# A mixture-of-experts and attention kernel: sine and amplitude rows behind the logits, expert loads re-ordered around the first gather, tile rows turned ahead of the gate products, one hidden copy a step later

## The chip, the cores and the metric

The kernel runs on one core of a Trainium2 chip. The engines have names in the profile: PE is TensorE (matrix products; PEld are its weight loads), DVE is VectorE, ACT is ScalarE, POOL is GpSimd, SP is SyncE, which issues most transfers. The metric is device time in microseconds (us), the median of several runs.

## The reference, cut to what matters

```python
xn = layernorm(x)                                   # x: 8 batches x 512 rows x 256
# attention: q, k, v, o are low rank: (xn @ basis.T) @ (amp * cos(phase)).T, 32 harmonics, 16 heads
attn_out = holo(softmax(q @ k.T * scale) @ v, "o")
# experts: 8 experts, the best 2 for each row, hidden width 352
scores = softmax(xn @ gate_w.T);  top 2, normalised, times 2.5
expert = silu(x @ w_gate[e]) * (x @ w_up[e]) @ w_down[e]
# a shared expert of hidden width 704 for every row
shared = silu(xn @ sw_gate) * (xn @ sw_up) @ sw_down
out = x + attn_out + expert_sum + shared
```

## The kernel before, in words

Each engine has its own program, written out by hand. Semaphores tie them together: an engine runs its list in order, and a wait holds everything behind it. A float32 value is split into a high part (rounded to the format that TensorE multiplies) and a low part, and each product is made of three. So every weight needs a copy on ACT (the high part, `high_part(e)`) and a subtraction on DVE (the low part, `low_part(e)`).

The work goes through these stages.

1. **Rows and logits.** For each of 8 batches ACT normalises 4 tiles of 128 rows (`normal(b)`), PE turns them (`turn_rows`), ACT copies the high part of the turned columns (`columns_high`), DVE subtracts the low one (`columns_low`), PE makes the router's logits (`logits(b)`), ACT copies them (`keep_logits`), PE turns them back (`turn_logits`). On the side the cosines of the low-rank weights are made: `angles()` on DVE, a sine on ACT, `thrice()` on DVE (amplitude times sine, three copies), `turn_thrice()` on PE into PSUM banks, two copies `w_rows` on ACT and `small_rows()` on DVE.
2. **Routing.** DVE alone finds the two best experts of each row (to `hot_b`), PE counts them, DVE works out slots.
3. **Token list.** For each batch DVE writes two one-hot arrays (`one_hots`: `at_tile1`, `at_row`), ACT scales one by the token numbers (`token_ids(b)`), and PE sums 8 small products into one bank (`invert(b)`). The arrays have two buffers, so that batch b waits for batch b-2. Then DVE casts the bank to `token_of`, and `a_done` is raised. In the same stretch PE and ACT make the low-rank rows of the first attention batch (`project_first`, `rest_first` on PE, `project_high`, `project_low` on ACT).
4. **Expert tiles.** POOL gathers 128 rows for each of 71 tiles by `token_of`, four ahead. For tile s PE turns the rows (`turn_x`), ACT and DVE split them (`x_out`, `x_low`), PE makes gate and up products (`gate_up`, 12 products of 352 columns), ACT and DVE make the hidden values (`silu`, `hidden`), PE turns them (`turn_h`) and makes `down` (9 products of 256 columns). The order on PE is gate_up(s), turn_x(s+1), turn_h(s-1), down(s-2). The first 8 tiles wait for `lo_dve`, one expert for each. The rest run in a loop of 8 tiles.
5. **Attention and shared expert.** 8 batches x 4 groups x 8 steps. In a step ACT takes the exponent of 1024 scores (`exponent`, one PSUM pair `st_pair`, so that the next `score_T` on PE waits for it), DVE the maxima of the next group, and PE fills in products of the shared expert. The hidden rows of that expert come in blocks. Block 1 (`BOTH`, 64 rows) is gated in step 5 of group 1, and ACT copies its high part (`hidden_high`) one step later.

SP's list sets the order of the transfers. `KEPT` is 6: experts 0 to 5 are loaded in front of the `qk_rows` stores (the first attention batch), experts 6 and 7 once the first gather has landed (`c_x[0]`), into a buffer of their own.

## Time and profile before

| | us |
|---|---|
| median of 3 runs (lowest, highest) | 1013.65 (1013.43, 1014.67) |
| the profiled execution: time, span | 1018.13, 1016.3 |
| PE busy | 931.1 (92%) |
| DVE, ACT, POOL busy | 641.8, 570.7, 310.5 |
| mean granted TensorE clock | 0.95 of full |

The span runs from the first to the last instruction; the time is 1.83 us more. Rows of a timeline begin with the start and the duration, and a number in square brackets behind a row is how long the engine stood idle before it, and on what. The granted clock is a share of 2.4 GHz: 1.0 is that, 0.50 is 1.2 GHz.

### The profile page before, as it was taken

To read this page: it belongs to the slowest core of one execution; us is meant where nothing else is said; L and a number is where in the kernel's file an instruction comes from. 1 tells how busy PE (TensorE), PEld (TensorE's weight loads), DVE (VectorE), ACT (ScalarE), POOL (GpSimd) and SP (SyncE) were. 2 spreads that over 40 slices of the span, in tenths; PEclk is the share of its full clock that TensorE was granted. 3 is DMA by queue.
4 is the path that set the end of the run, shared out by engine and by line. 5 is a ranking of instruction groups with operands and counts; after the bars stand their busy time and mean duration, and the time that the engine had idled before them with its cause. 6 is when DMAs were issued, how large, how long until landed. Compare 5 with 4: busy or idle time off the path is not lost.

```text
span 1016.3 us, 17567 instructions
## 1 busy us (share of the span) xinstructions
PE 931.1 (92%) x5563; PEld 610.3 (60%) x5564; DVE 641.8 (63%) x978; ACT 570.7 (56%) x900; POOL 310.5 (31%) x297
## 2 busy tenths in 40 slices
PE   4755999999999968899999999999999999999998
PEld 2445999999999952345545545545545545545546
DVE  7777744334444446666776776676776776786753
ACT  5756544444444434556566566566566566665563
POOL 1003222222222106135235235135235235135232
PEclk9765999999999985799999999999999999999999
DMA  9977255222222235354565465565565565544220
GB/s 317 363 232 270 83 161 144 72 72 67 76 67 69 63 114 160 104 137 139 156 165 147 148 156 143 160 148 147 165 150 135 174 147 143 170 105 96 57 63 22
DMA packets 94079, 139.90 MB, mean 138 GB/s; under 512 B 18200, under 2 KB 51488, under 8 KB 92992
## 3 DMA queue, kind: packets, MB, share of 16 engines
q1 hardware_dynamic: 87328, 121.25, 41.6%
q0 software_dynamic: 6480, 17.70, 5.9%
q8 instruction: 36, 0.59, 0.2%
q14 instruction: 27, 0.22, 0.1%
q10 hardware_dynamic: 208, 0.14, 0.0%
HBM read 79.24 MB, written 54.71 MB: 132 GB/s over the span
## 4 chain that ended last, share of the span: by engine, by line
PE 66%; DVE 12%; issue 8%; ACT 8%; DMA 2%; POOL 2%; SPq 2%; ACTq 0%; POOLq 0%
PE bank L1335 9%; PE st_pair L1346 8%; PE bank L1241 8%; PE s_pair L1223 7%; PE bank L1401 7%; PE st_pair L1223 7%; PE bank L1358 6%; PE s_pair L1297 5%; ACT prob L1023 4%; DVE top L1727 4%; PE bank L1231 2%; DVE h_f L1751 2%; PE bank L1206 2%; ACT x_n L834 1%; PE bank L1368 1%
## 5 line engine op out<-in xcount | busy, mean ns | idle before, releaser
L1727 DVE TENSOR_REDUCE top<-s_pair 128x2 f32<-128x1024 f32 x252 | 308.6, 1225 | 149.7 <-PE s_pair L1297 148.5
L1023 ACT ACTIVATE prob<-st_pair 128x1024 f32<-128x1024 f32 x256 | 260.7, 1018 | 174.9 <-PE st_pair L1346 173.0
L758 POOL TENSOR_TENSOR h_T<-h_f,h_T 128x512 fp32r<-128x512 f32 x40 | 51.4, 1285 | 364.6 <-ACT h_T L1005 364.6
L736 POOL DMA_INDIRECT xg<-xn_rows,token_of x71 | 70.0, 986 | 269.8 <-PE bank L1206 187.5
L1346 PEld LDWEIGHTS st_pair<-q_rows,k_rows 50*128 50x128 f32 x512 | 49.1, 188 | 168.2 <-ACT prob L1023 122.4
L1346 PE MATMUL st_pair<-q_rows,k_rows 50*128 50x512 f32 x512 | 131.7, 510 | 15.9 <-ACT prob L1023 10.4
L1335 PE MATMUL bank<-xT_b,w_sh 128*128 128x512 f32 x528 | 145.7, 411 | 0.0
L1358 PE MATMUL bank<-prob,v_ones 128*32 128x512 f32 x1024 | 140.7, 622 | 0.0
L1297 PE MATMUL s_pair<-k_rows,q_rows 48*128 48x512 f32 x504 | 113.7, 443 | 6.3 <-DVE top L1727 5.7
L1335 PEld LDWEIGHTS bank<-xT_b,w_sh 128*128 128x128 f32 x528 | 94.1, 191 | 31.4 <-issue 12.0
L1241 PE MATMUL bank<-w_exp,c_hT 128*128 (+1 forms) x639 | 93.6, 291 | 1.0 <-ACT c_y L946 1.0
L1223 PE MATMUL s_pair<-w_exp,xg_T 128*128 x432 | 78.1, 331 | 11.1 <-issue 9.8
L1401 PE MATMUL bank<-w_sh,h_T 128*128 128x256 f32 (+1 forms) x544 | 84.4, 297 | 0.1
L1241 PEld LDWEIGHTS bank<-w_exp,c_hT 128*128 128x128 f32 (+1 forms) x639 | 80.6, 190 | 1.4 <-issue 1.4
L1401 PEld LDWEIGHTS bank<-w_sh,h_T 128*128 128x128 f32 (+1 forms) x544 | 71.5, 190 | 12.7 <-DVE h_f L1751 3.5
L1223 PEld LDWEIGHTS s_pair<-w_exp,xg_T 128*128 128x128 f32 x432 | 70.3, 192 | 13.5 <-issue 13.5
L1223 PE MATMUL st_pair<-w_exp,xg_T 128*128 x420 | 74.8, 328 | 1.2 <-DVE xg_T L1690 1.2
L1223 PEld LDWEIGHTS st_pair<-w_exp,xg_T 128*128 128x128 f32 x420 | 68.4, 192 | 1.6 <-issue 1.5
L1681 DVE TENSOR_TENSOR c_h<-c_sil,s_pair 128x352 f32<-128x352 f32 x36 | 18.8, 521 | 79.7 <-PE s_pair L1223 77.7
L1297 PEld LDWEIGHTS s_pair<-k_rows,q_rows 48*128 48x128 f32 x504 | 50.5, 193 | 27.4 <-DVE top L1727 16.4
L769 POOL DMA_INDIRECT y_b<-expert_rows,slot_of x64 | 61.1, 955 | 18.4 <-issue 17.7
L1681 DVE TENSOR_TENSOR c_h<-c_sil,st_pair 128x352 f32<-128x352 f32 x35 | 18.2, 521 | 64.0 <-PE st_pair L1223 63.8
(226 smaller groups left out, 1143.4 us busy)
## 6 DMA issues: line engine op xcount, KB each, us to landing
qk_rows<-qk_hi SPq DMA_DIRECT2D x56, 256.0 KB
q_rows<-qk_rows SPq DMA_DIRECT2D x64, 192.0 KB
k_rows<-qk_rows SPq DMA_DIRECT2D x56, 192.0 KB
expert_rows<-c_y SPq DMA_DIRECT2D x71, 128.0 KB, 1.7
xn_T_split<-x_T SPq DMA_DIRECT2D x8, 1024.0 KB, 5.6
xT_b<-xn_T_split SPq DMA_DIRECT2D x32, 256.0 KB, 4.7
qk_rows<-qk_lo SPq DMA_DIRECT2D x28, 256.0 KB
x_all<-in_L_attn_x_dram SPq DMA_DIRECT2D x8, 512.0 KB, 8.1
```

What stands on the lines that cost most here:

```text
L736: pool.indirect_dma_start(xg[s % 4][:, :], None, xn_dram, bass.IndirectOffsetOnAxis(token_of[:, s:s + 1], 0)).then_inc(c_x[s % 4], 16)
L758: pool.tensor_tensor(h_T[0:m, LO, f, :], h_f[q % 2][0:m, :], h_T[0:m, HI, f, :].bitcast(F32), ALU.subtract).then_inc(p_h, 1)
L769: pool.indirect_dma_start(y_b[:, t, k, :], None, y_dram, bass.IndirectOffsetOnAxis(slot_of[:, k, of(b) * TPB + t:of(b) * TPB + t + 1], 0)) ...
L1023: act.activation(prob[kt % 2][:, 2 * jp:2 * jp + 2, :].rearrange("p j l -> p (j l)"), st_pair[:, :], ACT.Exp, scale=HD ** -0.5).then_inc(a ...
L1223: ins = pe.matmul(gu_bank[i % 2][n][:, 0:F], xg_T[i % 2][:, a * KT + k, :], w, start=(m == 0 and k == 0), stop=(m == 2 and k == KT - 1))
L1241: ins = pe.matmul(y_bank[:, 0:D], c_hT[i % 2][0:n, a, k, :], w, start=(m == 0 and k == 0), stop=(m == 2 and k == FT - 1))
L1297: ins = pe.matmul(score_pair(b, g, v)[:, i * 512:(i + 1) * 512], q_rows[g][r:r + 48, jp, qt * P:(qt + 1) * P], k_rows[g][r:r + 48, jp, :], ...
L1335: ins = pe.matmul((g_bank, u_bank)[n][:, :], w_sh[:, a, o:o + P], xT_bs[b % 3][:, c, k, :], start=(i == 0), stop=(i == 5))
L1346: ins = pe.matmul(st_pair[:, i * 512:(i + 1) * 512], k_rows[g][r:r + QK_ROWS, jp, kt * P:(kt + 1) * P], q_rows[g][r:r + QK_ROWS, jp, :], s ...
L1358: ins = pe.matmul(ot_bank[32 * j:32 * j + 32, :], v_ones[:, kt, 4 * g + j, :], prob[kt % 2][:, j, :], start=(kt == 0), stop=(kt == TPB - 1))
L1401: ins = pe.matmul((g_bank, u_bank)[t % 2][:, 0:D], h_T[0:m, a, f, t * P:(t + 1) * P], w_sh[0:m, c, S_GU + f * D:S_GU + (f + 1) * D], start ...
L1727: dve.tensor_reduce(top[g % 2][:, :, jp, qt], score_pair(b, g, v)[:, :].rearrange("p (i k) -> p i k", i=2), AX_X, ALU.max).then_inc(d_max, 1)
```

## The change

Seven things are edited.

- The sine goes behind `keep_logits(6)`. `turn_thrice` goes behind the first low-rank products on PE, into banks 4 and 5, the `w_rows` copies behind `e_lo` on ACT, and `small_rows` behind `hot_b` on DVE.
- SP loads expert 0 ahead of the first low-rank rows, and `high_part(0)` comes before the first projections.
- `token_ids(0)`, `token_ids(1)` on ACT and `invert(0)`, `invert(1)` on PE go in between the last projections.
- `EARLY` is 4: experts 4 to 7, not 6 and 7, are loaded behind the first gather, and their high parts follow the first four tiles on ACT.
- PE turns tile s+1 ahead of gate_up(s), ACT and DVE split it ahead of silu(s) and hidden(s).
- `hidden_high(BOTH)` comes one step later in the attention.

```diff
+        EARLY = NE - 4
+        def unit_two(b, g, t):
+            return (b, g, t - 2) if t >= 2 else after(b, g, -1) + (STEPS - 2 + t,)
+        thrice_bank = [bank[4], bank[5]]
@@ SP
             sp.wait_ge(consts, 1)
+            load_expert(0)
...
-            for e in range(KEPT):
+            for e in range(1, EARLY):
                 load_expert(e)
...
             sp.wait_ge(c_x[0], 16)
-            for e in range(KEPT, NE):
+            for e in range(EARLY, NE):
                 load_expert(e)
@@ ACT
             normal(7)
-            act.wait_ge(angle_ok, 1)
-            act.activation(angle, angle, ACT.Sin).then_inc(sin_done, 1)
             columns_high(6)
...
             keep_logits(6)
-            act.wait_ge(pe_prep, 2)
-            for i in range(2):
-                ins = act.activation(w_rows[...], bank[i][0:96, :], ACT.Copy)
-            ins.then_inc(rows_hi, 1)
+            act.wait_ge(angle_ok, 1)
+            act.activation(angle, angle, ACT.Sin).then_inc(sin_done, 1)
             keep_logits(7)
...
             act.activation(e_lo[0][0:96, :], rest_bank[0:96, :], ACT.Copy).then_inc(d_r, 1)
+            (the w_rows copies, from thrice_bank)
+            high_part(0)
...
             project_low(2)
+            token_ids(0)
             project_high(3)
+            token_ids(1)
             project_low(3)
-            high_part(0)
-            for b in range(NB):
+            for b in range(2, NB):
                 token_ids(b)
...
             def step(s, i, first=False, last=False):
-                silu(s, i)
                 if not (last and i == END - 1):
                     x_out(s + 1, (i + 1) % 4)
+                silu(s, i)
...
-                    if what == "up" or what == "gate" and i == BOTH:
+                    what, c, i = unit(*unit_two(b, g, t)) if t else (None, None, None)
+                    if what == "gate" and i == BOTH:
+                        hidden_high(c, i)
+                    what, c, i = unit_before(b, g, t)
+                    if what == "up":
                         hidden_high(c, i)
@@ PE
             low_rank_first()
+            turn_thrice()
             pe.wait_ge(hot_ok, 1)
...
+            invert(0, 0, first=True)
             project_first(3)
+            invert(1, 1)
             rest_first(3)
...
+                    if not (last and i == run - 1):
+                        turn_x(s + i + 1, (i + 1) % 4)
                     gate_up(s + i, i, at[i + 2])
-                    if not (last and i == run - 1):
-                        turn_x(s + i + 1, (i + 1) % 4)
@@ DVE
             columns_low(7)
-            small_rows()
...
             dve.tensor_tensor(hot_b[:, :, :], ...).then_inc(hot_ok, 1)
+            small_rows()
             dve.wait_ge(count_ps, 1)
...
             def step(s, i, first=False, last=False):
-                hidden(s, i)
                 if not (last and i == END - 1):
                     x_low(s + 1, (i + 1) % 4)
+                hidden(s, i)
```

Three places of the order are shown, each as it stood and as it stands.

ACT at the end of the first stage, before: the lines are those of the kernel before; `raw_all` is the sine's operand, `lg_rows` are the copies of `keep_logits`, `x_T` the two copies of `columns_high`.

```order
L870 ACT_TABLE_LOAD
L870 ACTIVATE raw_all<-raw_all 128x256 [waits angle_ok]
L842 ACTIVATE x_T<-st_pair 128x512 [waits xT_stored2,lg_turned,xt_ps]
L842 ACTIVATE x_T<-st_pair 128x512
L873 ACTIVATE neg<-ident_f 128x128 [waits consts]
L848 ACTIVATE lg_rows<-bank 16x512 [waits lg_ps,lg_turned]
L842 ACTIVATE x_T<-bank 128x512 [waits xT_stored3,lg_turned,xt_ps]
L842 ACTIVATE x_T<-bank 128x512
L848 ACTIVATE lg_rows<-bank 16x512 [waits lg_ps,lg_turned]
L879 ACTIVATE w_rows<-s_pair 96x512 [waits pe_prep]
L879 ACTIVATE w_rows<-s_pair 96x512
L848 ACTIVATE lg_rows<-bank 16x512 [waits lg_ps,lg_turned]
```

The same place in the changed kernel:

```order
L848 ACTIVATE x_T<-st_pair 128x512 [waits xT_stored2,lg_turned,xt_ps]
L848 ACTIVATE x_T<-st_pair 128x512
L854 ACTIVATE lg_rows<-bank 16x512 [waits lg_ps,lg_turned]
L848 ACTIVATE x_T<-bank 128x512 [waits xT_stored3,lg_turned,xt_ps]
L848 ACTIVATE x_T<-bank 128x512
L879 ACTIVATE neg<-ident_f 128x128 [waits consts]
L854 ACTIVATE lg_rows<-bank 16x512 [waits lg_ps,lg_turned]
L882 ACT_TABLE_LOAD
L882 ACTIVATE raw_all<-raw_all 128x256 [waits angle_ok]
L854 ACTIVATE lg_rows<-bank 16x512 [waits lg_ps,lg_turned]
```

The table load and the sine have moved from ahead of the last columns to ahead of the last `lg_rows` copy, and the `w_rows` copies are gone from here.

PE around the last projections and the token list, before: `at_tile,at_row` are the products of `invert`, eight for a batch.

```order
L1172 MATMUL st_pair<-e_hi,neg 128x512 [waits a_qk] x2
L1172 MATMUL bank<-x_T,neg 128x512 [waits a_qk]
L1167 MATMUL bank<-e_qk,w_rows 128x512 [waits d_qk]
L1168 MATMUL st_pair<-e_qk,w_rows 128x512
L1172 MATMUL st_pair<-x_T,neg 128x512 [waits a_qk]
L1181 MATMUL st_pair<-at_tile,at_row 128x72 [waits d_qk,inv_ok,inv_row]
L1181 MATMUL st_pair<-at_tile,at_row 128x72 x7
```

The same place in the changed kernel:

```order
L1179 MATMUL st_pair<-e_hi,neg 128x512 [waits a_qk] x2
L1179 MATMUL bank<-x_T,neg 128x512 [waits a_qk]
L1188 MATMUL st_pair<-at_tile,at_row 128x72 [waits d_qk,inv_ok,inv_row]
L1188 MATMUL st_pair<-at_tile,at_row 128x72 x7
L1174 MATMUL bank<-e_qk,w_rows 128x512 [waits d_qk]
L1175 MATMUL st_pair<-e_qk,w_rows 128x512
L1188 MATMUL st_pair<-at_tile,at_row 128x72 [waits inv_ok,inv_row]
L1188 MATMUL st_pair<-at_tile,at_row 128x72 x7
L1179 MATMUL st_pair<-x_T,neg 128x512 [waits a_qk]
```

The fourth projection now stands behind the first batch's token products, and its rest behind the second's.

ACT in steps 4 to 7 of group 1 of an attention batch, before: `prob` are the exponents of steps 5, 6 and 7, `h_T<-h_f 64x512` is `hidden_high(BOTH)`.

```order
L1023 ACTIVATE prob<-st_pair 128x1024 [waits b_st]
L988 ACTIVATE top_T<-bank 8x512 [waits m_in0,b_mt]
L999 ACTIVATE h_f<-bank 64x512 [waits p_h,b_g]
L1023 ACTIVATE prob<-st_pair 128x1024 [waits b_st,b_pv]
L1005 ACTIVATE h_T<-h_f 64x512 [waits b_dn,d_hf]
L1023 ACTIVATE prob<-st_pair 128x1024 [waits b_st]
```

The same place in the changed kernel:

```order
L1028 ACTIVATE prob<-st_pair 128x1024 [waits b_st]
L993 ACTIVATE top_T<-bank 8x512 [waits m_in0,b_mt]
L1004 ACTIVATE h_f<-bank 64x512 [waits p_h,b_g]
L1028 ACTIVATE prob<-st_pair 128x1024 [waits b_st,b_pv]
L1028 ACTIVATE prob<-st_pair 128x1024 [waits b_st]
L1010 ACTIVATE h_T<-h_f 64x512 [waits b_dn,d_hf]
```

The exponent of step 7 and the copy have changed places.

## Rows read from the trace of the kernel before

**Rows 1.** Busy time in two stretches: engine busy and instructions, clock, DMA share.

```profile
200.00:300.00 100.00, 96.39 (x704) 95.24 (x703) 40.24 (x81) 45.37 (x108) 25.35 (x28) 1.00 0.22 71
...
657.92:734.35 76.43, 74.80 (x436) 38.91 (x434) 56.24 (x69) 47.53 (x63) 28.46 (x26) 1.00 0.58 157
```

**Rows 2.** Timeline of ACT at the end of the first stage.

```profile
40.58 1.28 ACT L870 ACT_TABLE_LOAD   x1
...
42.20 1.06 ACT L842 ACTIVATE x_T<-st_pair 128x512 fp32r<-128x512 f32 x2
```

**Rows 3.** Timeline of PE there: logits, turned logits, `turn_thrice` (L1102).

```profile
39.54 1.11 PE L1120 MATMUL bank<-x_T,gate_T 128*16 128x512 f32 x4
...
43.97 0.61 PE L1128 MATMUL bank<-ident_f,lg_rows 16*128 16x16 f32 x4 [2.26 <-ACT lg_rows L848]
44.64 1.89 PE L1120 MATMUL bank<-x_T,gate_T 128*16 128x512 f32 x4
46.33 1.91 PE L1102 MATMUL s_pair<-ident_f,raw_all 128*96 128x128 f32 x8
...
48.70 1.85 PE L1120 MATMUL bank<-x_T,gate_T 128*16 128x512 f32 x4
```

**Rows 4.** Busy time from 44 to 46 us, columns as above.

```profile
44.00:46.00 2.00, 1.94 (x8) 0.98 (x9) 2.00 (x4) 0.87 (x2) 0.00 (x0) 0.50 0.68 254
```

**Rows 5.** Timeline of DVE: `small_rows`, the first logits row, the counted totals.

```profile
49.38 1.28 DVE L1563 TENSOR_TENSOR w_rows<-s_pair,w_rows 32x512 fp32r<-32x512 f32 x2 [2.73 <-ACT w_rows L879]
51.68 0.69 DVE L1603 TENSOR_REDUCE lg<-bank 128x256 f32<-128x512 f32 x1 [1.02 <-PE bank L1128]
...
61.23 0.42 DVE L1620 COPY totals<-s_pair 128x256 f32<-128x256 f32 x1 [0.70 <-PE s_pair L1189]
```

**Rows 6.** Timelines of ACT, DVE and PE in the token list.

```profile
68.05 2.01 ACT L821 ACTIVATE w_exp<-w_exp 128x2176 fp32r<-128x2176 f32 x1
69.96 2.54 ACT L905 ACTIVATE at_tile<-at_tile,token_id 128x144 fp32r<-128x144 f32 x8
...
66.67 0.76 DVE L1654 TENSOR_TENSOR at_tile<-iota_s,slot_q 128x576 f32<-128x576 f32 x1
...
71.37 14.44 PE L1181 MATMUL st_pair<-at_tile,at_row 128*128 128x72 f32 x64 [3.85 <-DVE at_row L1656]
...
86.27 0.23 DVE L1671 CAST token_of<-st_pair 128x72 int32<-128x72 f32 x1
```

**Rows 7.** Timelines of POOL, DVE and PE at the first gather, and landing times of ten gathers.

```profile
86.79 3.29 POOL L736 DMA_INDIRECT xg<-xn_rows,token_of  x1 [81.34 <-DVE token_of L1671]
90.39 1.81 POOL L736 DMA_INDIRECT xg<-xn_rows,token_of  x1 [0.30 <-issue]
...
86.62 4.76 DVE L1575 TENSOR_TENSOR w_exp<-w_exp 128x2176 fp32r<-128x2176 f32 x2
...
94.37 0.66 PE L1206 MATMUL bank<-ident_f,xg 128*128 128x128 f32 x2 [8.55 <-DMA xg<-xn_rows,token_of]
...
DMA to landing us min/median/max: 2.6/5.2/7.4
```

**Rows 8.** Timeline of PE, gate products of tiles 0 to 2; landing of experts 6, 7.

```profile
96.21 3.88 PE L1223 MATMUL s_pair<-w_exp,xg_T 128*128 x12 [1.18 <-DVE xg_T L1690]
...
101.67 3.69 PE L1223 MATMUL st_pair<-w_exp,xg_T 128*128 x12 [1.15 <-DVE xg_T L1690]
...
106.65 2.20 PE L1223 MATMUL s_pair<-w_exp,xg_T 128*128 x12 [0.75 <-issue]
...
DMA to landing us min/median/max: 4.3/6.0/7.8
```

**Rows 9.** Timelines of ACT, DVE and PE at step 7 of group 1, fourth attention batch.

```profile
660.95 0.63 ACT L1005 ACTIVATE h_T<-h_f 64x512 fp32r<-64x512 f32 x1 [1.56 <-DVE h_f L1751]
...
660.94 1.23 DVE L1727 TENSOR_REDUCE top<-s_pair 128x2 f32<-128x1024 f32 x1
...
662.63 0.50 PE L1346 MATMUL st_pair<-q_rows,k_rows 50*128 50x512 f32 x2 [0.90 <-ACT prob L1023]
```

More of the change, by code:

```diff
@@ L868, in _ @@
             normal(7)
+            columns_high(6)
+            keep_logits(5)
+            columns_high(7)
+            act.wait_ge(consts, 2)
+            act.activation(neg[:, :], ident_f[:, :], ACT.Copy, scale=-1.0)
+            keep_logits(6)
             act.wait_ge(angle_ok, 1)
             act.activation(angle, angle, ACT.Sin).then_inc(sin_done, 1)
-            columns_high(6)
-            act.wait_ge(consts, 2)
-            act.activation(neg[:, :], ident_f[:, :], ACT.Copy, scale=-1.0)
-            keep_logits(5)
-            columns_high(7)
-            keep_logits(6)
-            act.wait_ge(pe_prep, 2)
-            for i in range(2):
-                ins = act.activation(w_rows[:, 2 * i:2 * i + 2, :].rearrange("p n d -> p (n d)"), bank[i][0:96, :], ACT.Copy)
-            ins.then_inc(rows_hi, 1)
             keep_logits(7)
@@ L888, in _ @@
             act.activation(e_lo[0][0:96, :], rest_bank[0:96, :], ACT.Copy).then_inc(d_r, 1)
+            act.wait_ge(pe_prep, 2)
+            for i in range(2):
+                ins = act.activation(w_rows[:, 2 * i:2 * i + 2, :].rearrange("p n d -> p (n d)"), thrice_bank[i][0:96, :], ACT.Copy)
+            ins.then_inc(rows_hi, 1)
+            high_part(0)
             def project_high(n):
@@ L924, in _ @@
                 act.wait_ge(xT_stored[j], XT_STORED[j])
-            for e in range(1, KEPT - 1):
+            for e in range(1, EARLY):
                 high_part(e)
@@ L1101, in turn_thrice @@
                     for k in range(KT):
-                        ins = pe.transpose(bank[i // 2][0:96, (i % 2) * D + k * P:(i % 2) * D + (k + 1) * P],
+                        ins = pe.transpose(thrice_bank[i // 2][0:96, (i % 2) * D + k * P:(i % 2) * D + (k + 1) * P],
                                            w_thrice[:, i * KT + k, :, :].rearrange("p r h -> p (r h)"), ident_f[:, :])
@@ L1139, in _ @@
                 logits(b - 1)
-            turn_thrice()
             turn_logits(NB - 2)
@@ L1195, in _ @@
                 rest_first(n)
+            invert(0, 0, first=True)
             project_first(3)
+            invert(1, 1)
             rest_first(3)
-            for b in range(NB):
-                invert(b, b % 2, first=b == 0, last=b == NB - 1)
+            for b in range(2, NB):
+                invert(b, b % 2, last=b == NB - 1)
             def turn_x(s, i):
@@ L1561, in small_rows @@
                 for i in range(2):
-                    src = bank[i][32:64, :]
+                    src = thrice_bank[i][32:64, :]
                     ins = dve.tensor_tensor(w_rows[32:64, 2 * i:2 * i + 2, :].rearrange("p n d -> p (n d)"), src,
```

9 lines of the change are left out of this document (3 added, 6 removed).

## The prediction, made blind

> **What bounds the kernel now.** I read the page first: PE is busy for most of the span. Then I cut the span into stages with the view of busy time by stretches. In the loop of expert tiles PE works 96.39 us of 100 and its weight loads 95.24; in one whole attention batch it works 74.80 us of 76.43 [rows 1]. In both a change can win only what PE idles, 3.6 and 1.6 us there. The stretch up to about 110 us is another kind: there PE waits, and the end of the stage is set by a chain that passes from engine to engine. I followed it in the timelines, engine by engine, and noted at each place who ends last. The chain is: ACT's sine, PE's logits, DVE's routing, the token list, the first gather, the first three tiles. After that all work is queued on PE, so a microsecond won on this chain is won at the end, and one lost there is lost.
>
> **The change part by part.** Negative is faster.
>
> *Logits: -3.8.* Before, ACT loads the sine's table at 40.58 and starts the columns of batch 6 only at 42.20 [rows 2]. These 1.62 us are on the chain: PE idles 2.26 us until 43.97 [rows 3]. After, the sine stands where ACT waits for the last logits, 1.6 us of work beside a turn and a logits product of PE (0.6 + 1.9); that hides it, and without that cover it would cost 1.6. The second piece is `turn_thrice`, 1.91 us on PE [rows 3]. It partly covered ACT's copy of the logits (about 0.6, half of the two copies' 1.06 in [rows 2] and a handover), which PE now waits for, so it gives about 1.0. That makes 1.62 + 1.0 = 2.6. The third is the clock. After the idle 2.26 us the granted clock is 0.50 [rows 4], 1.2 GHz, and the two logits take 1.89 and 1.85 us against 1.11 at the high level [rows 3]. In the changed order PE has no gap there longer than about 0.6 us, so I expect it to keep 2.4 GHz: 0.78 + 0.74 + about 0.2 for the short turns gives 1.7 more. The bounds are 2.6 and 4.3; I take 3.8, nearer to the high clock.
>
> The Trainium skill (TensorE: Matmul & The Clock Gate, Part 4: PE-mode transpose) says that transposes do not count as PE work for the clock. By that rule the turns between the logits would not hold the clock up, and this term would be 2.6. No row here separates the two; it is a rival below.
>
> *small_rows: +0.6.* Its 1.28 us moves to behind `hot_b`, on the routing chain. DVE idled 0.70 there for the counts [rows 5], so 0.6 shows. The bounds are 0 and 1.3. In its old place it cost nothing, since DVE idled 1.02 behind it.
>
> *Token list: +2.0.* I count from T, DVE's first one-hot (66.67 before). Before, ACT is at the high part of expert 0 until 69.96, PE starts the products at 71.37 = T+4.7, runs them without a gap for 14.44 us, 1.8 a batch, to T+19.1, and the cast starts at 86.27 = T+19.6 [rows 6]. After, the high part is out of the way, and PE can start at T+2.1 (one-hot 0.76, token numbers 1.3, a half of 2.54). But now a ping-pong follows. First batch to T+3.9; the fourth projection behind it, 0.45 (a quarter of the 1.89 in [rows 3]), T+4.4; ACT's copy 0.5, T+4.9; only then the second token numbers, 1.3, T+6.2; second batch, T+8.0; rest product 0.45 and ACT's copy 0.5, T+9.0; third token numbers, T+10.3. From here six batches at 1.8, T+21.1, and the cast at T+21.6. That is 2.0 later, though it was begun earlier. The bounds are -2.2, if only the stall before the third batch goes, and +2.5.
>
> *First gather: -2.5.* PE idles 8.55 us for the first gathered tile [rows 7]. Before, experts 4 and 5 stand ahead of the `qk_rows` stores, which so run on beside the gather. After, 2.2 MB less lies in front, and the stores are done. The gather takes 7.4 us there and the fastest of ten 2.6 [rows 7]. Not all of the difference goes: of the 7.4 us POOL itself spends 3.29, and the next gather 1.81, where DVE is busy in the same stretch for 4.76 us with the low parts of experts 0 and 1 [rows 7]. These stay where they are, so POOL's part stays. What is left behind it, 7.4 - 3.3 = 4.1, should fall to about 1.6 (I take the fastest gather less about 1 of POOL's). The bounds are 0 and -3.9.
>
> The Trainium skill (SBUF — State Buffer, Who interferes with whom) states that a DVE operation with two SBUF inputs and a GpSimd operation that reads SBUF shut each other out for a whole instruction. The trace agrees in size: 3.29 is one low part of 2.4 and a short gather. Had the queue alone made the 7.4 us, the whole gain would be 4.8.
>
> *Second gather: +0.8.* PE now turns tile 1 ahead of the first gate product. So that product waits for the second gather, which POOL ends 1.81 + 0.3 us after the first [rows 7], and for a turn of 0.66; against the split of tile 0 that it waits for anyway (1.18, [rows 8]) some 0.8 is new. It cannot be under 0; if the experts' transfers slow that gather, it is 3.
>
> *Gaps between the first tiles: -2.0.* The second and third gate product waited 1.15 and 0.75 us for their split tiles [rows 8]. With the turn a tile ahead these 1.9 go, and PE may reach the high clock sooner, as it works without a break. From the fourth tile DVE's low parts pace both kernels. The bounds are 0 and -3.3. Four experts now come behind the gather, where two did. One landed in 4.3 to 7.8 us with two in flight [rows 8]; with a tile needing 3.7 us or more, each expert should land just before its tile, as DVE and ACT work one behind another.
>
> *Loop of 63 tiles: 0.* PE does the same products, and a turn changes sides with a product. PE idles almost nowhere [rows 1].
>
> *Attention: -4.2.* ACT waits 1.56 us for DVE's hidden rows with the next exponent behind it, and PE then stands 0.90 us for that exponent [rows 9]. After, the exponent runs in that wait. PE's next score into `st_pair` can start 0.90 sooner, but its next product for the maxima needs the bank that DVE reads from 660.94 for 1.23 us, to 662.17 [rows 9]. That holds part of the gain; I put what is left at 0.5. The copy itself is late by about 0.6 us, and only DVE's low part waits for it, which stands behind that maximum anyway. All 8 batches have this place: 8 x 0.5, and 0.2 more for the first, is 4.2. The bounds are 0 and 8 x 0.9 = 7.2.
>
> The sum is -3.8 + 0.6 + 2.0 - 2.5 + 0.8 - 2.0 + 0 - 4.2 = -9.1 us. The profiled execution took 1018.13 us (span 1016.3), which is 4.5 above the median of the runs, so I take the difference over: 1018.13 - 9.1 = 1009.0 for such an execution, 1013.65 - 9.1 = 1004.6 for the median.
>
> **The rivals.**
> - *The front gives nothing:* the ping-pong, the wait for the second gather and the late experts eat all that the logits win. The row for it is the 14.44 us of token products, which can only shift as a block [rows 6]; against it stands the 8.55 us gather. Attention alone is left: 1013.65 - 4.2 = 1009.5.
> - *The attention gives nothing:* the half microsecond is taken up at the next wait for DVE's maxima. For it speaks the bank held to 662.17, against it that PE has hardly any other gap in the batch [rows 1, 9]. The front is -4.9: 1008.8.
> - *The clock stays low in the logits:* -9.1 + 1.2 = -7.9, 1005.8, with a chance of 0.2 inside the likeliest case's 0.52. The clock rose earlier in this stage behind mixed turns and products, which speaks against it. The Trainium skill's rule on transposes, named above, would bring this case about.
> - *More than I count:* 0.9 in each batch and no ping-pong loss, or the full clock gain: -7.2 - 4.9 - 0.5 = -12.6, 1001.1.
> - *Slower:* turning ahead costs in the loop. The loop has 63 tiles, and PE has no idle time to take up anything. If the first gate product lost 0.18 us of overlap in each tile (a weight load behind two short turns instead of behind nine products), that is 63 x 0.18 = 11.3, and 1013.65 - 9.1 + 11.3 = 1015.9. It decides from 0.14 a tile. Nothing in the rows speaks for it.
> - *No change:* the same loss at about 0.14 a tile, or two of the cases that give nothing together.
>
> **How the numbers follow.** A measurement of this kernel tells about 0.2%, 2.0 us, from no change. The likeliest case, -9.1 with its own range of 1002.5 to 1007 (the clock at either level included), has 0.52. Nothing from the front has 0.13, nothing from the attention 0.12, more than counted 0.10, no change 0.07, slower 0.06. The range from 1001 to 1010 holds the first four but for the far end of "more", about 0.85. Faster by over 0.2% is 0.87, within it 0.07, slower 0.06.
>
> The Trainium skill (TensorE: Matmul & The Clock Gate, What's actually happening) says that the clock's rise depends on a free-running phase and varies between runs of one kernel. It is a reason not to trust the term of the logits to better than its bounds.
>
> **What would show it.** In the changed kernel's profile: the first routing operation on DVE (lg<-bank) at 47.4 to 49.1 us; PE's token products broken into three pieces, the last of 6 batches; the cast of `token_of` near 85; POOL's first gather still about 3.3 us; the gap before the first turned tile near 5 to 6 us; in the loop the same 704 products in 100 us as before; in each attention batch no 0.9 us gap at step 0 of group 2, and a batch of 75.9 instead of 76.4. I am wrong if the loop's tiles are longer, if ACT waits for an expert's transfer in the first tiles, or if the batches keep 76.4.

## The result, and the profile of the changed kernel

The changed kernel takes 1006.74 us, the median of 6 runs (1003.02 to 1008.13). Before, it took 1014.92, now over 6 runs (1013.43 to 1017.66). The ratio is 0.9911, with a 95% interval of 0.9893 to 0.9929: 9.0 us less, between 7.2 and 10.9. That is the side, the size and the range that were forecast. The terms that make it up are not, as the marks will show.

The page of the changed kernel (busy us, share of the span, instructions; then the granted clock in 40 slices; then the chain that ended last):

```profile
PE 934.8 (93%) x5563; PEld 612.9 (61%) x5564; DVE 642.7 (64%) x978; ACT 568.5 (57%) x900; POOL 319.5 (32%) x297
...
PEclk9965999999999975999999999999999999999999
...
PE 68%; DVE 15%; ACT 8%; issue 4%; DMA 3%; SPq 1%; POOL 1%; ACTq 0%
```

The profiled execution took 1006.07 us, its span is 1004.3. PE was busy for 931.1 us before and is for 934.8 now, so its idle time fell from 85.2 to 69.5 us.

The end of the first stage, as in [rows 2, 3, 5]: PE, ACT and DVE.

```profile
42.59 1.89 PE L1128 MATMUL bank<-x_T,gate_T 128*16 128x512 f32 x4
44.28 1.41 PE L1119 MATMUL bank<-ident_f,x_n 128*128 128x128 f32 x8
...
45.96 1.11 PE L1128 MATMUL bank<-x_T,gate_T 128*16 128x512 f32 x4
47.74 0.42 PE L1136 MATMUL bank<-ident_f,lg_rows 16*128 16x16 f32 x4 [0.68 <-ACT lg_rows L854]
...
49.00 0.42 ACT L882 ACTIVATE raw_all<-raw_all 128x256 f32<-128x256 f32 x1
...
50.42 0.69 DVE L1612 TENSOR_REDUCE lg<-bank 128x256 f32<-128x512 f32 x1
...
59.29 1.28 DVE L1573 TENSOR_TENSOR w_rows<-bank,w_rows 32x512 fp32r<-32x512 f32 x2
```

The sine is out of PE's way, and a logits product takes 1.11 us, where [rows 3] had 1.89. But note the first row: its product takes 1.89 us, as those at a granted clock of 0.50 in [rows 3] and [rows 4]. So PE was at the low clock until about 44 here, in code that the change doesn't touch. (The view's own clock column gives 1.00 from 20 to 50 us in this profile and in attn_only; for this stretch I go by the durations.)

The token list and the first tiles on PE, as in [rows 6 to 8]:

```profile
68.28 1.89 PE L1188 MATMUL st_pair<-at_tile,at_row 128*128 128x72 f32 x8 [2.33 <-ACT at_tile L912]
...
72.74 1.89 PE L1188 MATMUL st_pair<-at_tile,at_row 128*128 128x72 f32 x8 [1.57 <-ACT at_tile L912]
...
77.21 10.84 PE L1188 MATMUL st_pair<-at_tile,at_row 128*128 128x72 f32 x48 [1.99 <-ACT at_tile L912]
94.16 0.66 PE L1216 MATMUL bank<-ident_f,xg 128*128 128x128 f32 x2 [6.12 <-DMA xg<-xn_rows,token_of]
97.46 0.69 PE L1216 MATMUL bank<-ident_f,xg 128*128 128x128 f32 x2 [2.64 <-DMA xg<-xn_rows,token_of]
97.80 3.87 PE L1233 MATMUL s_pair<-w_exp,xg_T 128*128 x12
```

The reader sees the forecast ping-pong: two single batches of 8 products, each behind a wait for ACT, and then the block of 48. Then come the two waits for gathers. The first is 6.12 instead of 8.55, the second is new. POOL, DVE's cast and ACT in the same stretch:

```profile
89.02 3.29 POOL L742 DMA_INDIRECT xg<-xn_rows,token_of  x1 [83.57 <-DVE token_of L1681]
92.61 1.81 POOL L742 DMA_INDIRECT xg<-xn_rows,token_of  x1 [0.30 <-issue]
...
88.50 0.23 DVE L1681 CAST token_of<-st_pair 128x72 int32<-128x72 f32 x1
...
101.79 2.02 ACT L827 ACTIVATE w_exp<-w_exp 128x2176 fp32r<-128x2176 f32 x1 [1.38 <-DMA w_exp<-in_L_ffn_w_down_dram]
```

The loop and one attention batch, columns as in [rows 1], and step 7 of group 1 in that batch, as in [rows 9]:

```profile
200.00:300.00 100.00, 97.89 (x710) 96.61 (x709) 41.03 (x82) 44.88 (x109) 25.52 (x27) 1.00 0.23 72
648.00:724.04 76.04, 75.13 (x436) 38.92 (x434) 56.22 (x69) 47.62 (x63) 28.48 (x26) 1.00 0.56 152
```

```profile
651.03 0.63 ACT L1010 ACTIVATE h_T<-h_f 64x512 fp32r<-64x512 f32 x1
...
651.03 1.23 DVE L1737 TENSOR_REDUCE top<-s_pair 128x2 f32<-128x1024 f32 x1
...
651.75 0.50 PE L1356 MATMUL st_pair<-q_rows,k_rows 50*128 50x512 f32 x2
652.31 0.51 PE L1307 MATMUL s_pair<-k_rows,q_rows 48*128 48x512 f32 x2
```

The copy waits for nothing. PE's score (651.75) stands without a gap, and the product for the next maxima starts at 652.31, as DVE's reduction ends (652.26): the hold that the prediction named. The batch takes 76.04 us, not 76.43. In the loop PE makes 710 products in 100 us, where it made 704. That was forecast as no change, and it is the largest surprise.

### The profile page after: what moved, and what is told of

It is laid out like the page before. It is cut to its first block, busy times and chain, and to the rows that moved or that the text cites. A ratio compares the mean times of both kernels' runs of the same rounds, so it can differ in the third digit from the quotient of the medians.

```text
span 1004.3 us, 17510 instructions
## 1 busy us (share of the span) xinstructions
PE 934.8 (93%) x5563; PEld 612.9 (61%) x5564; DVE 642.7 (64%) x978; ACT 568.5 (57%) x900; POOL 319.5 (32%) x297
## 4 chain that ended last, share of the span: by engine, by line
PE 68%; DVE 15%; ACT 8%; issue 4%; DMA 3%; SPq 1%; POOL 1%; ACTq 0%
PE bank L1345 10%; PE bank L1251 8%; PE st_pair L1356 8%; PE bank L1411 7%; PE s_pair L1233 7%; PE st_pair L1233 7%; DVE top L1737 6%; PE bank L1368 6%; PE s_pair L1307 5%; ACT prob L1028 4%; DVE h_f L1761 2%; PE bank L1241 2%; PE bank L1216 2%; PE bank L1378 1%; ACT x_n L840 1%
## 5 line engine op out<-in xcount | busy, mean ns | idle before, releaser
L742 POOL DMA_INDIRECT xg<-xn_rows,token_of x71 | 78.9, 1112 | 254.8 <-PE bank L1216 169.7
L1368 PE MATMUL bank<-prob,v_ones 128*32 128x512 f32 x1024 | 138.1, 612 | 0.0
L1233 PE MATMUL s_pair<-w_exp,xg_T 128*128 x432 | 80.6, 336 | 0.0
L1233 PE MATMUL st_pair<-w_exp,xg_T 128*128 x420 | 77.0, 332 | 0.0
L949 ACT ACTIVATE c_hT<-bank 128x384 fp32r<-128x384 f32 x71 | 34.9, 492 | 55.2 <-PE bank L1241 55.2
L1700 DVE TENSOR_TENSOR xg_T<-bank,xg_T 128x256 fp32r<-128x256 f32 x71 | 30.1, 424 | 54.8 <-ACT xg_T L939 54.8
```

The lines of the kernel that those rows point to most:

```text
L742: pool.indirect_dma_start(xg[s % 4][:, :], None, xn_dram, bass.IndirectOffsetOnAxis(token_of[:, s:s + 1], 0)).then_inc(c_x[s % 4], 16)
L1233: ins = pe.matmul(gu_bank[i % 2][n][:, 0:F], xg_T[i % 2][:, a * KT + k, :], w, start=(m == 0 and k == 0), stop=(m == 2 and k == KT - 1))
L1368: ins = pe.matmul(ot_bank[32 * j:32 * j + 32, :], v_ones[:, kt, 4 * g + j, :], prob[kt % 2][:, j, :], start=(kt == 0), stop=(kt == TPB - 1))
```

## The experiments

Twelve more kernels ran, four on each of three chips, and each is compared with the kernel before on the same chip. On the first two chips the kernel before took 1015.0 and 1015.4 us; on the third it took 1069.9, so the kernels that ran there are compared by ratio. "Changed kernel" is the one under study. This table has the starts in us, in each profiled execution, of DVE's first logits row, its first one-hot, its cast to `token_of`, PE's first turned tile, gate products 0 and 3, and DVE's first attention maximum (the last three lines are from the third chip).

| kernel | row | one-hot | cast | turn 0 | gate 0 | gate 3 | maximum | ratio, 95% |
|---|---|---|---|---|---|---|---|---|
| before | 51.68 | 66.67 | 86.27 | 94.37 | 96.21 | 110.32 | 368.07 | |
| changed | 50.42 | 66.06 | 88.50 | 94.16 | 97.80 | 109.04 | 364.05 | 0.9911 (.9893-.9929) |
| attn_only | 51.05 | 66.05 | 85.63 | 93.91 | 95.75 | 109.90 | 367.68 | 0.9949 (.9928-.9971) |
| attn_undone | 50.05 | 65.69 | 88.13 | 93.79 | 97.33 | 108.84 | 364.19 | 0.9972 (.9951-.9992) |
| tokens_back | 50.05 | 65.70 | 84.41 | 90.13 | 93.34 | 104.84 | 360.24 | 0.9871 (.9841-.9901) |
| turn_back | 50.26 | 65.92 | 88.36 | 94.11 | 95.95 | 109.14 | 366.82 | 0.9943 (.9917-.9969) |
| sine_only | 50.09 | 65.72 | 86.34 | 94.67 | 96.52 | 108.88 | 366.68 | 0.9992 (.9975-1.001) |
| early6 | 50.37 | 66.01 | 88.45 | 94.20 | 97.50 | 108.85 | 363.86 | 0.9921 (.9901-.9941) |
| gather_free | 50.14 | 65.78 | 88.23 | 91.86 | 97.43 | 108.23 | 363.18 | 0.9910 (.9889-.9930) |
| both | 49.28 | 64.93 | 83.64 | 89.34 | 91.40 | 103.03 | 358.27 | 0.9881 (.9854-.9908) |
| tokens_early6 | 47.64 | 63.28 | 81.68 | 89.85 | 91.90 | 103.12 | 358.10 | 0.9887 (.9864-.9910) |
| held | 50.48 | 66.12 | 84.83 | 88.41 | 91.57 | 104.69 | 359.77 | 0.9899 (.9884-.9914) |
| five | 47.58 | 63.22 | 81.28 | 87.53 | 89.66 | 103.19 | 358.23 | 0.9888 (.9863-.9913) |

**The later copy alone (attn_only).** The kernel before, with one edit:

```diff
-                    if what == "up" or what == "gate" and i == BOTH:
+                    (hidden_high(BOTH) by unit_two, one step later)
```

> The kernel before with one edit alone: the copy of the 64 hidden rows one step later. Theory A (each edit is worth its own term, the rest of the difference between the two profiles is the clock's phase): the gap of 0.9 us in front of step 0 of group 2 goes, a batch from one such copy to the next is 0.4 to 0.5 us shorter (76.0 instead of 76.4), the median is 3 to 4 us under the kernel before, ratio 0.9965. Rival R (the attention took all of the 8 us by which the last two thirds of the span shrank in the profiles): about 8 us, ratio 0.992. Rival N (the half microsecond is lost again at the next wait): under 1 us, ratio 1.000.

Measured 1008.79 us, 6.2 under before by the medians, 5.2 by the ratio (2.9 to 7.3). The front keeps its shape: the marks are within 0.7 us of before, and gate 3 to the first maximum takes 257.78, as before (257.75).

**The later copy undone (attn_undone).** The changed kernel without that edit.

> The changed kernel without the later copy, all else as changed. Theory A: batches of 76.4 again, the gap of 0.9 us back, the time 3 to 4 us over the changed kernel, ratio to the kernel before 0.9945. Rival R: ratio 0.999. Rival N: 0.991 as the changed kernel.

Measured 1011.09 us, ratio 0.9972: 0.61% above the changed kernel's 0.9911, some 6 us. In the records a batch goes from 76.0 to 76.4 or 76.5 us, and the first batch has a gap of its own. PE in batch 0, first without the later copy, then in the changed kernel:

```profile
422.58 0.50 PE L1353 MATMUL st_pair<-q_rows,k_rows 50*128 50x512 f32 x2 [2.45 <-ACT prob L1028]
```

```profile
421.19 0.51 PE L1356 MATMUL st_pair<-q_rows,k_rows 50*128 50x512 f32 x2 [0.98 <-ACT prob L1028]
422.26 0.50 PE L1307 MATMUL s_pair<-k_rows,q_rows 48*128 48x512 f32 x2 [0.56 <-DVE top L1737]
```

Seven batches at 0.4 and 0.9 here are 3.7 us. The medians say 5 to 6, with 3.7 inside both intervals; a gain of 8 from this edit alone (rival R) is outside attn_only's. What may lie between is below, under the clock.

**Projections ahead of all token products again (tokens_back).** The changed kernel, with

```diff
             project_high(3)
             project_low(3)
             for b in range(NB): token_ids(b)         # ACT
...
             project_first(3)
             rest_first(3)
             for b in range(NB): invert(b, ...)       # PE
```

> The changed kernel with the last projection and its rest ahead of all token products on PE, and their copies ahead of all token numbers on ACT, as in the kernel before; the high part of expert 0 stays early. Theory A (the ping-pong costs): PE runs the 64 token products without a gap from 2.1 us behind the first one-hot, the cast of token_of starts 17 us behind it instead of 22.4, so 5 us sooner, and the time is about 5 us under the changed kernel, ratio to before 0.986. Rival Q (the gather takes it back: the qk_rows stores still run then, until about 85 us): the cast comes 5 us sooner but the first gather takes 7 us instead of 5, and the time is only 2 to 3 us under the changed kernel, ratio 0.9885. Rival N (VectorE or the products' own pace is the limit): nothing, 0.991.

Measured 1001.32 us, ratio 0.9871 (0.9841 to 0.9901), the lowest of the study. By the ratios that is about 4 us under the changed kernel, though the two intervals overlap a little; the marks of the profiles say the same. PE:

```profile
69.51 14.45 PE L1186 MATMUL st_pair<-at_tile,at_row 128*128 128x72 f32 x64 [1.95 <-DVE at_row L1662]
90.13 0.66 PE L1212 MATMUL bank<-ident_f,xg 128*128 128x128 f32 x2 [6.17 <-DMA xg<-xn_rows,token_of]
```

The products are one block again, from one-hot + 3.8 to + 18.3, and the cast comes at + 18.7. In the changed kernel it came at + 22.44 (in all five profiles with that order, 22.44 or 22.45), before at + 19.60. So the interleaving costs 2.85 us against before, and 3.7 against this order. Theory A had the products start 2.1 us behind the one-hot and the cast come at + 17; both are 1.7 us later than that. Rival Q fell: PE waits 6.17 us for the gather, as in the changed kernel (6.12). The gain stays to the end: gate 3 is 4.2 us sooner than in the changed kernel, the first maximum 3.8.

**Tiles turned where they were (turn_back).** The changed kernel, with the old order of turn, split and hidden values.

> The changed kernel with the old order of a tile on PE, ACT and DVE (gate products, then the next tile's turn). Theory A (the turn ahead costs 1.8 us of wait for the second gather, wins 2.9 on the next gaps and about 0.25 us in each pass of 8 tiles): the first gate product 1.2 us behind the split of tile 0, gaps of about 1 us back before the second and third, a pass of the loop of 29.8 us instead of 29.55 with an idle stretch of 1.2 instead of 0.7 us at its start; in all 2.5 to 3.5 us over the changed kernel, ratio 0.994. Rival P (turning ahead is worth nothing or costs): 0.991 or under.

Measured 1008.00 us, ratio 0.9943 (0.9917 to 0.9969), 3.2 us above the changed kernel by the ratios, whose intervals overlap, and 2.8 by the first maximum of the profiles. Up to gate 3 the two are level: 109.14 and 109.04. The difference is in the loop. The chain of work between 120 and 260 us, rows of "issue" (PE waits for nothing recorded), in this kernel and in the changed one:

```profile
157.29 1.34 issue
187.22 1.20 issue
```

```profile
156.35 0.78 issue
185.95 0.71 issue
```

They stand 29.9 and 29.6 us apart, a pass of the loop's 8 tiles: PE stands idle for 1.2 us at the seam, where one pass ends and the next begins, if a pass begins with a gate product, and for 0.7 if it begins with two short turns. The rest of the pass gives half of it back: the passes differ by 0.3 us.

**The sine and the amplitude rows alone (sine_only).** The kernel before, with the sine, `turn_thrice`, the `w_rows` copies and `small_rows` moved.

> The kernel before with one part of the change: the sine behind the seventh lg_rows copy, turn_thrice into banks 4 and 5 behind the first low-rank products, the w_rows copies behind e_lo, small_rows behind hot_b. Theory A (each edit has its own term): the first routing row comes 7.9 us after the end of the last normalised rows, not 11.1; small_rows gives back 0.65; the token products may start later, as the w_rows copies stand ahead of the projections on ACT and the fourth batch of them is still one block: about -2 to -3 us in the median, ratio 0.9975. Rival P (the phase of the clock made the logits short in the changed kernel): PE is again at 0.50 in the logits, the distance is 9.5 or more, ratio 0.999. Rival H (all is lost in the token list, whose start the ACT copies set): the distance is 7.9, but the cast comes no sooner than 45.7 us behind the last normalised rows, ratio 1.000.

Measured 1014.95 us, ratio 0.9992 (0.9975 to 1.001): no change that can be told. Theory A's 0.9975 stands at the very edge of the interval, so its -3 is excluded and its -2 is unlikely. The last two logits products took 1.10 us each, so PE was at the high clock there, and rival P falls. The first logits row came 8.5 us behind the last normalised rows (before 11.1, in attn_only with the old order 8.6), the one-hot at 65.72. But the token numbers of batch 0 wait for expert 0's high part on ACT, which ends at 70.1, as before; so the cast is at 86.34, where it was (86.27), and the first turn at 94.67 (94.37). What was won ahead of the one-hot is lost in the token list, as rival H says. H had the cast come no sooner than 45.7 us behind the last normalised rows (as before); it came 44.8 behind them, since those rows were ready 1.0 us later in this execution.

**Six experts in front again (early6).** The changed kernel with `EARLY` at 6, and the high parts where they stood before.

> The changed kernel with six experts again ahead of the qk_rows stores and the first gather, and their high parts on ACT where they stood before. Theory A: the first tile is turned 7.6 us after POOL starts the gather, not 5.1; ACT's waits of 1.38 and 0.56 us for experts 4 and 5 go, and the gate products from the second on are paced by DVE's low parts; net +1.5 to +2.4 us against the changed kernel, ratio to before 0.993. Rival L (late experts cost as much as the sooner gather wins): the first turn is 2.4 us later, but gate(3) comes at the same distance from the cast as in the changed kernel (20.5 us), ratio 0.991. Rival G (the gather's length has nothing to do with the queue): the first turn stays at 5.1.

Measured 1006.39 us, ratio 0.9921 (changed 0.9911): level. Theory A fell. The first tile is turned 5.2 us behind POOL's start, as in the changed kernel (5.1). That is rival G's number, but tokens_early6 below shows that the queue does matter. ACT's waits for experts went, but gate 3 is at 108.85 against 109.04, so late experts cost nothing that shows. I had put the shorter gather down to the 2.2 MB of experts. The DMA's traffic tells it better (last two columns: busy share, GB/s). In the changed kernel:

```profile
82.00:84.00 2.00, 2.00 (x10) 1.91 (x10) 2.00 (x4) 1.53 (x6) 0.00 (x0) 0.50 0.53 204
...
86.00:92.00 6.00, 2.05 (x10) 1.88 (x9) 5.76 (x13) 5.73 (x4) 2.98 (x1) 0.50 0.00 0
```

with six experts in front:

```profile
90.00:92.00 2.00, 0.00 (x0) 0.00 (x0) 2.00 (x2) 2.00 (x2) 2.00 (x1) 0.50 0.33 126
```

and in the kernel with the sine alone:

```profile
90.00:92.00 2.00, 0.00 (x0) 0.00 (x0) 1.45 (x1) 1.47 (x1) 1.70 (x2) 0.50 0.65 238
92.00:94.00 2.00, 0.00 (x0) 0.00 (x0) 0.00 (x0) 0.00 (x0) 1.39 (x3) 0.50 0.66 241
```

Traffic at 201 to 205 GB/s, half of the DMA's share, is the `qk_rows` stores. It stops near 84.7 in the changed kernel and near 91 with six experts in front; with the sine alone it runs past 92, the gathers beside it. POOL is done with the first gather at 92.3, 92.3 and 90.2. From that to PE's first turn it takes 1.85 and 1.94 us where the stores are over, 4.5 where they still run. So what counts is whether the stores end before POOL does. By how much they do makes no difference here: 7.6 us in the changed kernel, about 1 with six experts in front.

**Six experts in front, token list fast (tokens_early6).** tokens_back with `EARLY` at 6. It tells whether `EARLY` is worth something once POOL is sooner.

> The run that took the token products back (cast near 84.4), with six experts instead of four ahead of the stores. Theory S: the stores end near 90.5 to 91, after POOL's own end (88.2), so the first tile is turned near 92.5, 7.6 us behind POOL's start, where it was 5.2 with four experts; gate(0) comes 2.3 us later than there, ratio to before 0.9895. Here EARLY is worth what it was not in the changed kernel, where POOL ended at 92.3, behind the stores in either order. Rival M (the number of experts in front never matters): the turn stays at 5.2, ratio 0.987.

Measured 1057.74 us on the third chip. The first turn came 7.65 us behind POOL's start (82.20), 4.4 behind POOL's end, as Theory S said; with four experts it was 5.2 and 1.9. The DMA while POOL ends (85.5) and behind it:

```profile
84.00:86.00 2.00, 0.00 (x0) 0.00 (x0) 2.00 (x2) 2.00 (x2) 1.70 (x2) 0.50 0.52 201
86.00:88.00 2.00, 0.00 (x0) 0.00 (x0) 0.79 (x1) 0.82 (x1) 1.70 (x2) 0.50 0.64 236
```

But of these 2.4 us only 1.3 are left at gate 0 (10.2 us behind the cast against 8.9), 1.0 at gate 3 and 0.6 at the first maximum, since the second gather has landed by then and turn 1 follows at once. The ratio, 0.9887, can't be told from tokens_back's 0.9871. The size of the landing was foreseen; what it is worth at the end is a quarter of the 2.3 that I named.

The Trainium skill (DMA: Bandwidth & Descriptors, Queues, rings and completion order) says that each DMA engine goes round between its queues, and that the write that reports a transfer lands only behind earlier writes of that engine, on any queue. By it a gather is reported late while stores are in flight, though it is not queued behind them. The 1.9 and 4.4 us agree with that in direction; no run here tells a late report from rows that come late themselves.

**Expert 0 loaded sooner (expert0_early).** sine_only with `load_expert(0)` ahead of the first low-rank rows. It asks which edit let the stores end sooner with six experts in front.

> The kernel with the sine moved alone, and expert 0 loaded ahead of the first low-rank rows. Theory S (the first gather lands 1.9 us after the later of two ends, POOL's own and the last qk_rows store's; loading expert 0 sooner fills an idle stretch of the queue, so that the stores end some 2 us sooner): POOL starts near 86.9 as in the run without this edit, and the first tile is turned 5.2 to 5.8 us later, not 7.8; gate(0) near 94.5 instead of 96.5, ratio to before 0.997. Rival K (it is the high part of expert 0, the projections or the token list that shortened the gather in the changed kernel): the first turn stays 7.8 us behind POOL's start, ratio 0.999.

Measured 1069.73 us, ratio 0.9989 (0.9973 to 1.0006): rival K's number, and that of sine_only; Theory S's 0.997 lies just outside. The profiled execution took 4237 us and its trace has no rows of this stretch, so whether the gather came sooner can't be seen. Which edit let the stores end sooner stays open.

**DVE held until the gather has landed (gather_free).** The changed kernel, with

```diff
+            dve.wait_ge(c_x[0], 16)
             low_part(0)
             low_part(1)
```

> The changed kernel with one more wait: DVE holds its low parts of experts 0 and 1 until the first gather has landed. Theory A (a DVE subtraction of two SBUF operands holds POOL's gather up): POOL's first gather takes about 0.95 us, not 3.29, the second 0.95, not 1.81, and the first tile is turned about 2.7 us after POOL's start, not 5.1. The two low parts (4.8 us) then begin 2.7 us later, so that gate(0), which needs the first, moves by 0 to +1.5 us; ratio to before 0.990 to 0.993. Rival C (a first gather is slow by itself, by cold code or its descriptors): POOL's first gather stays at 3.29.

POOL and DVE:

```profile
88.75 1.17 POOL L742 DMA_INDIRECT xg<-xn_rows,token_of  x1 [83.29 <-DVE token_of L1681]
90.23 0.95 POOL L742 DMA_INDIRECT xg<-xn_rows,token_of  x1 [0.31 <-issue]
...
92.74 2.31 POOL L742 DMA_INDIRECT xg<-xn_rows,token_of  x1 [0.30 <-issue]
...
91.80 4.76 DVE L1585 TENSOR_TENSOR w_exp<-w_exp 128x2176 fp32r<-128x2176 f32 x2 [3.26 <-issue]
```

Theory A holds: with DVE away POOL's first gather takes 1.17 us, not 3.29, the second 0.95, not 1.81, and the fourth now takes 2.31, where DVE's low parts run. The first turn is 3.1 us behind POOL's start. The Trainium skill (SBUF — State Buffer, Who interferes with whom) has this rule, and the run agrees. The time is level (1006.65 us, ratio 0.9910), because the low parts are late by as much: gate 0 at 97.43 against 97.80.

**Token list and the second low part (both).** tokens_back, with `low_part(1)` behind `x_low(0, 0)`.

> The changed kernel with the last projection and its rest ahead of all token products again, as before the change, and DVE's low part of expert 1 behind the split of the first tile instead of ahead of it. Theory A: cast 18.7 us after the first one-hot, as in the run that took the token products back alone. DVE is free after one low part, so the second gather takes 0.95 us on POOL, not 1.81; the first tile's low rows do not wait for the second low part: gate(0) 0.5 to 0.9 us nearer to the cast than 8.93 us, ratio to before 0.986. Rival D (DVE's low parts pace the first tiles, whatever their order): gate(3) keeps its 20.4 us from the cast, ratio 0.987, the same as without the swap.

Measured 1004.23 us. The second gather took 0.95 us, gate 0 came 7.8 us behind the cast, not 8.9; but gate 3 came 19.4 behind it, not 20.4 as in tokens_back, and 11.6 behind gate 0. The ratio, 0.9881, is level with tokens_back's. ACT waits 2.24 us for expert 4 here, as the tiles are now sooner than the experts behind the gather.

**Both, with DVE held (held), and with five experts in front (five).** The first adds the wait of gather_free, the second sets `EARLY` to 5.

> The run with both edits (token products back, expert 1's low part behind the first split), and DVE holds expert 0's low part until the first gather has landed. Theory A (the lock of DVE's subtraction and POOL): POOL's first gather takes 1.2 us, not 3.3, the first turn comes 3.1 us behind POOL's start, not 5.2; but low part 0 then begins at that landing, so gate(0) comes 2.4 + 0.8 us behind it: 6.7 us behind the cast instead of 7.8, and -1 us in the median, ratio 0.987 or better. Rival D (DVE's low parts pace the first tiles): gate(3) keeps its 19.4 us from the cast.

> The run with both edits, with five experts instead of four ahead of the stores. Theory S: the stores end near 87, where they ended 2.7 us sooner, still ahead of POOL's own end (87.5), so that the first turn stays 5.2 us behind POOL's start; ACT's wait of 2.24 us for expert 4 and PE's 0.82 us at the second tile go: gate(3) 11.0 us behind gate(0), not 11.6; ratio 0.987. Rival E: expert 5 is now the one that is late, gate(3) keeps its distance, ratio 0.988.

held took 1059.06 us, ratio 0.9899. POOL's 1.17 us and a first turn 3.1 us behind its start repeat. Gate 0 is 6.7 behind the cast as said, but gate 3 is 19.9 behind it, against 19.4 in the run both: that is rival D. five took 1057.80 us, ratio 0.9888. The first turn is 5.7 behind POOL's start, so the stores just reach into it, and ACT's wait moves from expert 4 to expert 5:

```profile
94.42 2.02 ACT L827 ACTIVATE w_exp<-w_exp 128x2176 fp32r<-128x2176 f32 x1 [2.13 <-DMA w_exp<-in_L_ffn_w_down_dram]
```

That is rival E's late expert. But gate 3 did not keep its 11.6 us from gate 0, as E had it: it came 13.5 behind. Gate products 0 and 1 took 3.88 and 3.87 us here, at the low clock; in the run both, product 1 took 2.21. None of the combinations can be told from tokens_back, which is the version to keep: some 4 us better than the change as it was made, with less moved.

## Why the prediction was right

The sum was -9.1 and the ratio says -9.0, but some of this is errors that cancel. Term by term, by the marks:

- **Logits, forecast -3.8: -1.3 between the two profiles.** This is the term that failed. The first routing row stands at 51.68 and 51.05 in the two profiles with the old order there, at 49.28 to 50.42 in the eight others outside the third chip. The row forecast for 47.4 to 49.1 came at 50.42. The step was "these 1.62 us are on the chain". They are only where PE comes to the end of `normal(7)` at the high clock. With PE at the low clock in the turns, the old order has no gap: in attn_only, whose code in this stretch is that of before, PE turns the last rows without waiting, and then

```profile
44.17 1.91 PE L1117 MATMUL bank<-ident_f,x_n 128*128 128x128 f32 x8
...
46.55 1.12 PE L1126 MATMUL bank<-x_T,gate_T 128*16 128x512 f32 x4
```

  The logits take 1.12 there with no edit at all. Both the 2.26 us gap and the 1.89 us products of [rows 3] were this execution's. The distance that is free of the earlier code is that from the end of the last normalised rows to the routing row: 11.1 us in the profile before, 8.6 in attn_only, 7.9 in the changed kernel, 7.8 to 8.6 in the eight others that were at the low clock. Two profiles of the third chip, five and tokens_early6, have the changed order and PE at the high clock there, as in before. The last normalised rows in before, then in five, and five's routing row:

```profile
38.50 2.06 ACT L834 ACTIVATE x_n<-x_all,rs 128x256 f32<-128x256 f32 x4
```

```profile
38.76 2.06 ACT L840 ACTIVATE x_n<-x_all,rs 128x256 f32<-128x256 f32 x4
47.58 0.69 DVE L1609 TENSOR_REDUCE lg<-bank 128x256 f32<-128x512 f32 x1
```

  From there to the routing row it is 11.12 us in before and 6.76 in five, and 47.58 and 47.64 lie where the row was forecast. So the term was priced rightly for the kind of execution it was read from (4.4 us), and wrongly as a term of the median: in the other kind the new order is worth 0.1 to 0.9. How often each kind comes, no run shows.
- **small_rows, +0.6: +0.65** (row to one-hot: 14.99 before, 15.63 to 15.65 where it was moved). Right.
- **Token list, +2.0: +2.85.** The mechanism was as worked out. Behind each single batch came a projection or its rest (0.77, not 0.45) and a wait for ACT of 1.57 and 1.99 us on PE, and DVE was caught too, with the one-hots of batches 3 and 4.
- **First gather, -2.5: -2.5** (cast to turn 8.10, now 5.66). The size is right, and so is POOL's unchanged 3.29. The reason given was half right: the stores had to be over, but six experts in front would have done as well, as early6 shows, because the token list had made POOL late.
- **Second gather, +0.8: +1.4 to +1.8** (first turn to gate 0: 1.84 in before and turn_back, 3.2 to 3.6 in those that turn ahead with the low parts where they were). PE now waits 2.64 us for the landing of the second gather; 0.9 of that is DVE's hold on POOL, which "both" took away.
- **Gaps between the first tiles, -2.0: -2.9** (gate 0 to gate 3: 14.11, now 11.24). But turn_back has gate 3 at the same time as the changed kernel, so the order of turning gives nothing by gate 3: what it wins in these gaps is what it loses in the line above.
- **Loop, 0: -2.6.** From gate 3 to the first attention maximum it is 257.75, 257.78, 257.80 and 257.68 us in the four profiles with the old order, and 254.95 to 255.40 in the six with the new one outside the third chip. I had said that PE idles almost nowhere in the loop and looked at no boundary of it; [rows 1] had 3.6 us of idle time in 100, and 1.2 of each 30 was this one. The rival in which turning ahead costs 0.18 us a tile fell.
- **Attention, -4.2: -3.7 by the records, -5 to -6 by the medians.** 0.4 in each batch against the forecast 0.5, for the reason given: the score starts sooner, and the product for the maxima waits for DVE.

By the marks the front with the loop is -4.0 at the first maximum (368.07 to 364.05; the mean of the changed kernel, attn_undone and early6 against that of before and attn_only gives -3.8), where -4.9 was forecast with no loop in it. Without the loop's 2.6 the front would have given about 1.3. That is close to the rival "the front gives nothing". It was luck that the loop, forecast at nothing, gave what the front fell short by. With the attention's 3.7 the marks add up to -7.7, inside the ratio's 7.2 to 10.9.

**The clock, and what stays open.** From the first maximum to the end it was 648.2 us before and 640.3 in the changed kernel, 8 us, of which the later copy explains 3.7. The executions differ in when the granted clock rises from 0.50 to 1.00 behind the start of attention, in stretches of 4 us: by 402 us in the changed kernel, by 414 in gather_free, by 418 in before, where it fell once more at 430. From the first maximum to the end it took 638.3 us in turn_back and 645.7 in "both", though both have the changed kernel's code there. One batch alone, from 574 to 651 us in the changed kernel, took 77.2 there and 76.2 in turn_back. So a profile's span says little here to better than some 4 us, and the two spans' difference (12.0) overstates the median's. Outside the third chip that stretch took 646.1 us in the mean of the three profiles with the old copy (643.4 to 648.2) and 640.8 in the mean of the seven with the later one. Those 5.3 us agree with the medians' 5 to 6 and not with the 3.7 counted in the batches. Whether the later copy also moves the clock in the first batch, the runs don't settle. The Trainium skill (TensorE: Matmul & The Clock Gate, What's actually happening) says that the clock rises by a free-running phase, so that runs of one kernel differ. The prediction named it, and still took the low clock of one execution as a cost to be removed.

## What to carry to other kernels

A gap that one profile shows at a low granted clock may be that execution's: take a second profile, or the same stretch of another version with the same code, before pricing it. When a product is put between the items of a producer-consumer chain, count every engine's turn, since each single item then pays the whole round. Look at the seam of a loop and at which instruction comes first behind it. For a transfer, ask whether others are still in flight when its engine is done issuing it; here it made no difference how long they had been over.

## What the runs showed of the hardware

- At the seam of PE's loop PE stands idle for 1.2 us (1.0 to 1.3) with gate products of 352 columns first, and for 0.7 (0.6 to 0.8) with two turns of 128 first, in every pass between 120 and 260 us of every profile.
- POOL's indirect gather takes 0.95 us alone. The first one took 3.29 when DVE's subtraction of two SBUF operands of 128x2176 (2.4 us) started just ahead of it, and 1.17 without that (gather_free, held).
- Where the 64 token products of 72 columns stand in one block, they keep PE busy for 14.4 us in a row, and the granted clock is 0.50 all through; so it is where they stand in three pieces. Behind them it rises in the gate products, in every profile.
- On the third chip the front and the loop take what they take elsewhere (255.0 us from gate 3 to the first maximum in all three profiles), but an attention batch takes 83 us, not 76. DVE and ACT each stop once in a batch for up to 7.6 us, and the record names no engine of this core. What DVE and ACT waited for in five between 500 and 900 us (in total, times, longest):

```profile
DVE top L1734 <- remote: 37.2, 5, 7.6
ACT prob L1027 <- remote: 29.4, 5, 7.2
```
